# Early-fusion transformer block on one core: in the ending, GpSimd adds the pair ahead's squares later, ScalarE moves squares, VectorE moves low parts

## What is computed

```python
def _ternary_linear(x, w):
    alpha = jnp.mean(jnp.abs(w))
    w_t = jnp.sign(w) * (jnp.abs(w) > 0.5 * alpha).astype(w.dtype)
    w_q = w + jax.lax.stop_gradient(w_t - w)
    rms = jnp.sqrt(jnp.sum(x * x, axis=-1, keepdims=True)) / jnp.sqrt(jnp.asarray(d, x.dtype))
    x_norm = x / (rms + EPS)
    return jnp.einsum('bsd,fd->bsf', x_norm, w_q)
...
h = _L0_tok_ref(x, W_embed, b_embed, pos_embed)
h = jnp.concatenate([h, txt], axis=1)
h = h + _L0_attn_ref(_layernorm(h, axis=-1), Wq, Wk, Wv, Wo, bo)
h = h + _L0_ffn_ref(_layernorm(h, axis=-1), w_up, w_down)
```

## Time and profile before

| what | value |
|---|---|
| median of 3 runs | 1940.74 us (1939.0 to 1941.06) |
| the profiled execution | 1944.63 us, of which the span from first to last instruction is 1942.6 us |
| busy share of the span | TensorE 96%, its weight loads 80%, VectorE 81%, ScalarE 68%, GpSimd 37% |
| chain that ended last, by engine | TensorE 66%, VectorE 21%, ScalarE 7%, issue 5% |
| mean granted TensorE clock | 0.985 |

### The profile page before, as it was taken

The page is one execution under the profiler, slowest core; times in us unless marked ns, Lnnn a source line. Parts: engine busy times, 40 slices in busy tenths (PEclk is TensorE's granted clock), DMA queues, the critical chain, the costliest instruction groups (busy, mean ns, idle before and its releaser), DMA issues.

```text
span 1942.6 us, 57163 instructions
## 1 busy us (share of the span) xinstructions
PE 1855.9 (96%) x24066; PEld 1556.0 (80%) x24066; DVE 1571.8 (81%) x2687; ACT 1311.8 (68%) x1920; POOL 726.2 (37%) x649
## 2 busy tenths in 40 slices
PE   5789999999999999999999999999999999999886
PEld 4668888888888888888888888888888888888765
DVE  4578888888888888888888888888888888888866
ACT  4447776677776676777676777667677667677654
POOL 1123333443433444333444343344433344433333
PEclk8899999999999999999999999999999999999988
DMA  4111122111112111112111111211111211111010
GB/s 142 27 47 30 52 57 57 52 38 36 51 52 57 52 44 42 40 52 57 52 54 39 33 52 56 57 52 38 37 50 52 57 52 50 38 38 40 31 35 25
DMA packets 66102, 93.54 MB, mean 48 GB/s; under 512 B 10082, under 2 KB 59718, under 8 KB 65592
## 3 DMA queue, kind: packets, MB, share of 16 engines
q1 hardware_dynamic: 65848, 89.90, 16.4%
HBM read 45.03 MB, written 14.94 MB: 31 GB/s over the span
## 4 chain that ended last, share of the span: by engine, by line
PE 66%; DVE 21%; ACT 7%; issue 5%; DMA 1%; POOL 1%; SPq 0%; POOLq 0%; ACTq 0%; DVEq 0%
PE dense L352 37%; PE score L352 18%; DVE gl L1029 7%; PE pvps L352 6%; DVE pT_lo L1005 4%; PE dense L409 3%; DVE rs L1015 2%; DVE mx L1057 2%; DVE qm L1071 2%; DVE mx L1059 2%; ACT sq L759 2%; ACT g L751 1%; PE dense L398 1%; ACT vp L784 1%; ACT pT_hi L718 1%
## 5 line engine op out<-in xcount | busy, mean ns | idle before, releaser
L1329 POOL TENSOR_SCALAR_AFFINE_SELECT pr<-pr 114x1368 f32<-114x1368 f32 x190 | 242.7, 1278 | 520.8 <-ACT pr L742 520.7
L742 ACT ACTIVATE pr<-score 114x1824 f32<-114x1824 f32 x190 | 320.8, 1689 | 59.6 <-PE score L352 59.3
L1029 DVE TENSOR_TENSOR gl<-g 128x456 f16<-128x456 f32 x256 | 229.8, 936 | 21.4 <-ACT g L751 20.7
L1341 POOL TENSOR_TENSOR acc<-acc,sq 128x456 f32<-128x456 f32 x190 | 237.4, 1250 | 22.8
L1057 DVE TENSOR_REDUCE mx<-score 114x4 f32<-114x912 f32 x192 | 211.6, 1102 | 30.7 <-PE score L352 30.7
L352 PE MATMUL dense<-wdn,g 128*114 128x256 bf16 x992 | 228.4, 278 | 1.5 <-ACT g L751 1.1
L352 PE MATMUL score<-qm,km 32*114 32x228 f32 (+1 forms) x4096 | 203.9, 324 | 21.3 <-DVE mx L1059 13.3
L352 PE MATMUL dense<-wdn,gl 128*114 128x256 bf16 x992 | 223.2, 273 | 0.0
L352 PEld LDWEIGHTS score<-qm,km 32*114 32x114 f32 x4096 | 157.8, 175 | 66.9 <-issue 57.5
L352 PE MATMUL score<-km,qm 32*114 32x228 f32 (+1 forms) x4096 | 202.6, 323 | 7.0 <-ACT pr L742 7.0
L1015 DVE RECIPROCAL rs<-rs 128x228 f32<-128x228 f32 x128 | 200.6, 1567 | 2.7 <-DMA cxraw<-cxraw 2.7
(11 more groups left out here) (145 smaller groups left out, 4541.5 us busy)
## 6 DMA issues: line engine op xcount, KB each, us to landing
pix<-x SPq DMA_DIRECT2D x32, 588.0 KB
sq<-x SPq DMA_DIRECT2D x32, 588.0 KB
rs<-cxraw SPq DMA_DIRECT2D x256, 57.0 KB, 2.0
cxraw<-cxraw SPq DMA_DIRECT2D x256, 57.0 KB, 2.0
out<-h SPq DMA_DIRECT2D x64, 228.0 KB
h<-txt SPq DMA_DIRECT2D x32, 64.0 KB, 4.6
km<-wqkvo SPq DMA_DIRECT2D x1, 1024.0 KB, 13.9
h<-w_upT SPq DMA_DIRECT2D x1, 1024.0 KB, 14.3
```

The costliest lines, as they stand in the source:

```text
L742: act(probs(pair, q), score[0:R, :, 0:4 * R], ACT.Exp, scale=float(HD) ** -0.5).then_inc(a["exp"], 1)
L1029: tt(gl[:, m], g[:, m], hi_view(g[:, m]), ALU.subtract).then_inc(v["gl"], 1)
L1329: nc.gpsimd.affine_select(out=blocks, in_=blocks, compare_op=ALU.is_ge, fill=0.0, base=0, pattern=[[0, 4], [0, n], [1, R]], channel_multip ...
L1341: tt(acc[:], sq[:, 0] if m == 1 else acc[:], sq[:, m % 4], ALU.add).then_inc(p["acc"], 1)
```

## The change

GpSimd makes variance_powers(L) before all seven accumulate(P), and not between the third and the fourth. VectorE makes all of P's gelu_lo ahead of second_moments(L); low_sums(P) moves behind the low parts of L's columns and the first two gelu_lo(L). ScalarE makes the squares 4 and 5 of P behind `normalized` of L, 6 and 7 behind the high parts, and all eight squares of L behind L's last gelu. TensorE makes sum_squares(P) behind six of L's eight `up` and not behind four.

```diff
@@ TensorE, ending
-                for m in range(4):
+                for m in range(6):
                     up(L, m)
                 sum_squares(P)
-                for m in range(4, 8):
+                for m in range(6, 8):
                     up(L, m)
@@ ScalarE, ending
                 eng.wait_ge(pe["pv"], count(4, L, 3))
-                for m in range(8):
+                for m in range(4):
                     square(P, m)
                 eng.wait_ge(pe["x2t"], count(2, P, 2))
                 normalized(h[0:R, L % 4], xn, sc2[:], nb2, a["xn2"], v["nb2"], L)
+                square(P, 4)
+                square(P, 5)
                 eng.wait_ge(pe["up"], count(8, P, 8))
                 hi_part("x2t", 0, xT2[0], L)
                 hi_part("x2t", 1, xT2[0], L)
+                square(P, 6)
+                square(P, 7)
                 for m in range(8):
                     gelu(L, m)
-                    if 3 <= m < 7:
-                        square(L, m - 3)
-                for m in range(4, 8):
+                for m in range(8):
                     square(L, m)
@@ VectorE, ending
                 gelu_lo(P, 4)
                 gelu_lo(P, 5)
-                second_moments(L)
                 gelu_lo(P, 6)
                 gelu_lo(P, 7)
+                second_moments(L)
                 scale_of(L)
-                low_sums(P)
                 lo_part("x2t", 0, xT2[0], xT2[1], L)
                 lo_part("x2t", 1, xT2[0], xT2[1], L)
-                for m in range(4):
+                gelu_lo(L, 0)
+                gelu_lo(L, 1)
+                low_sums(P)
+                for m in range(2, 5):
                     gelu_lo(L, m)
                 mean_squares(P)
-                for m in range(4, 8):
+                for m in range(5, 8):
                     gelu_lo(L, m)
@@ GpSimd, ending
                 causal(L, 5)
-                for m in range(1, 4):
-                    accumulate(P, m)
                 variance_powers(L)
-                for m in range(4, 8):
+                for m in range(1, 8):
                     accumulate(P, m)
                 accumulate(L, 1)
                 accumulate(L, 2)
```

## The result

The changed kernel takes 1942.70 us in the median of 20 runs (1939.20 to 1945.37), the kernel before 1940.28 us in the median of 20 (1935.46 to 1943.43). The ratio is 1.0015, 95% interval 1.0009 to 1.0022, that is +2.9 us (1.7 to 4.3). The forecast was 1943.4, +2.7 us on the median.

The account below looks back on a forecast made before the run. TensorE, busy 96%, bounds the steady steps; the very end hangs on GpSimd and TensorE nearly alike. Later additions of L (+2.5 us) and slow sum_squares (+0.2) gave +2.7 us on the median, 1943.4 us; range 1940.6 to 1945.6.

Parts of the forecast that it names:

- P's low parts first: VectorE's four gelu_lo of P ahead of second_moments(L): that moves +0.13 us, TensorE's wait shrinks from 4.92 to some 0.5.
- The normalization: L's powers, bias and xn: bias at 1911.6 instead of 1911.79, transposes start 1.7 us earlier.
- The low clock moves: TensorE's idle spell (4.65 us) and low clock shift from P's down matmuls to L's transposes and ups; 1.35 us lost.
- The low part beside an addition: VectorE's low part of L's columns while GpSimd adds P's fifth square: taken as no cost, up to +1.0 us in range.
- The gelus: L's last gelu on ScalarE ends at 1925.05 instead of 1925.34, a net gain of 0.3 us.
- The squares of L: Squares behind L's last gelu: GpSimd's first addition 2.95 us later, fifth done at 1933.4, +2.5 us.
- sum_squares at the low clock: TensorE's sixteen small matmuls at the end, after 3 us of waiting, may run slow: 0 to 0.4 us, 0.2 taken.
- the rival without a low clock: TensorE's clock does not fall or rises at once: +1.1 to +1.3 us, 1941.9; chance 0.17.
- the one with a long one: Low clock stays through most of L's up matmuls, at least until 1921.5: +4.0 us, 1944.7; chance 0.17.
- second_moments is late: Rival: P's two added low parts push second_moments(L) back 1.2 us instead of 0.13: +3.8 us, 1944.5; chance 0.10.
- TensorE sets the end: Rival: TensorE's down of L, not GpSimd's additions, decides the end: -2.2 us, 1938.5; chance 0.08.
- the hold-up behind the powers: VectorE's small operations behind L's powers, held up by a GpSimd addition: 1.10 us for four columns, taken to stay.

Follow-up runs that it names:

- e8: Changed kernel with three of P's GpSimd additions ahead of the powers again; ratio to before 1.0011, end +2.10 us against before.
- e1: Changed kernel with L's squares 0 to 3 between the gelus again, as before; ratio to before 0.9999, end -0.08 us.
- e2: Kernel before with all eight squares of L behind L's last gelu, nothing else changed; ratio to before 1.0012, end +3.07 us.
- e3: Changed kernel with 38 unread matmuls filling TensorE's idle spell ahead of L's transposes; ratio to before 1.0001, end +0.84 us.
- e4: e1 with the 38 unread matmuls of e3 as well; ratio to before 0.9996, end -1.01 us.
- e7: e6 without the unread matmuls; ratio to before 0.9998, end +0.90 us.
- e10: Changed kernel with GpSimd waiting for L's bias before the first of P's additions; ratio to before 1.0002, end +0.63 us.
- e6: e4 with P's root ahead of L's additions, four of these on GpSimd, three on VectorE, sum_squares(L) before the last down part; ratio to before 0.9985.
- e5: Kernel before with 38 unread matmuls in TensorE's idle spell ahead of P's down matmuls; ratio to before 0.9983, 1937.50 us against 1939.94.
- e11: e4 with e10's wait, 22 unread matmuls, L's squares behind gelu 5, sum_squares(P) behind all ups, mean_squares(P) before the last gelu_lo; ratio to before 1.0004.

## Why the prediction was right

Point by point, in times behind the mark:

- *P's low parts first.* Expected: second_moments +0.13 us, wait ahead of P's down 0.5 us at the high clock. Measured: 2.73 against 2.63, +0.10; 0.50 us; clock 1.00.
- *The normalization.* Powers 1.64 us (1.65, the median of before); bias 0.24 us earlier (expected 0.2). Transposes at 12.79 against 14.53: 1.74 us earlier, 1.7 expected.
- *The low clock moves.* The new idle spell is 4.48 us (4.65 expected), and the clock came back 5.2 us after the transposes began (5.15 taken, the middle of two cases; that it came so close is partly luck, as the other traces have 4.0 to 7.2). First up 15.19 against 16.46, -1.27 (-1.2).
- *The low part beside an addition.* Taken at nothing with up to 1.0 us in the range. All 64 took 620 to 634 ns again, the two of L (1911.47 to 1912.80) with GpSimd's additions (1910.27 to 1915.29) beside them:

```profile
L1011 DVE TENSOR_TENSOR xT_lo<-dense,xT_hi x64: 620/631/634, 160.9 to 1912.2; 128x456 f16<-128x456 f32 x64
```

  By the Trainium skill's rule (GPSIMD Engine Reference, section Specifications: contention for instructions with two SBUF inputs or in a two-port mode), this input from PSUM is exempt and gelu_lo is not. The traces agree on both sides: 0.63 here, and 5.14 against 2.25 us for four gelu_lo in e8.
- *The gelus.* The last one ends 0.31 us earlier (0.3).
- *The squares of L.* First addition +2.90 us (+2.95). From its start to the end of the fifth 7.13 us (7.3), before 7.73: fifth addition +2.30 us where +2.5 was written.
- *sum_squares at the low clock.* Taken at 0.2 us, measured at nothing: the clock was still 1.00 after 3.12 us without matmuls. With the 0.2 of the line above this is the whole difference between +2.7 and +2.29.

e1 and e2 show the squares as the cause from both sides, e3 the clock as the second term: 1.45 us, of which 0.33 lies ahead of the first up matmul (14.86 behind the mark in e3, 15.19 in the changed kernel) and 1.12 behind it, where 1.35 was taken. What the sum did not hold is that the two terms overlap: taken one at a time from the changed kernel, 2.37 (e1) and 1.45 (e3), taken together 3.30 (e4).

The number alone would prove little: the range of 1940.6 to 1945.6 also held the rival without a low clock (1941.9) and the one with a long one (1944.7), and the measured interval of 1.7 to 4.3 us even holds the second (+4.0). It is the rows that part them. The clock did fall (0.73 in 1908.00 to 1908.40). The rival that the low clock stays through most of the ups did not come about in the changed kernel's trace, but e7's 7.2 us is close to its 7.5. Of the signs named one failed: P's additions are not one row of seven, since GpSimd waits 1.65 us for P's fifth square behind the third; nothing hung on it. That second_moments is late and that TensorE sets the end are excluded by the rows above. Where the reasoning was thin is the hold-up behind the powers: the prediction had the row (1.10 us for four columns), named its cause, and let it stand as fixed. e10 shows that it could be had for one wait, and e8's expectation went wrong by the same omission.

What stays open: how long the low clock lasts in a given execution. The trace of each kernel is one draw (4.0 and 6.3 us before, 5.8 in e2, 5.2 after, 7.2 in e7), and e2's transposes moved by 0.87 us through it alone. That e6 is faster in the median than its end explains isn't settled either.

## What to carry to other kernels

When work is moved earlier, follow the last consumer and not the first: here the normalization came 1.7 us earlier, but the squares that the final factor needs were queued behind the gelus and came 2.9 us later. An idle spell of TensorE can cost more than the wait, namely matmuls at half pace behind it. The change moved the spell from P's down matmuls to L's transposes and up matmuls, where the slow pace cost 1.45 us (e3). Matmuls that nobody reads, put into the spell of the kernel before, gained 1.46 us in the ending (e5), where the reordering lost 2.29. For an ending of 40 us, measure from a mark inside the trace: the mark itself moved by up to 9.1 us between the traces here, and the edits moved the end by at most 3.1. One trace of each kernel still carries the clock's scatter, 0.87 us in e2.

## What the runs showed of the hardware that was not expected

- Two VectorE operations on 114 x 4 elements with SBUF inputs (0.16 us alone, e10 and e8) took 1.09 and 0.83 us when a GpSimd addition of 128 x 456 f32 had started ahead of them, and each ended as that addition ended (1906.07 and 1906.05, 1907.35 and 1907.33). How long they took was set by what was left of GpSimd's addition and not by their own 0.16 us.
- The clock's fall behind an idle TensorE is no function of the spell's length alone: in the changed kernel it was still at 1.00 when the sums came after 3.12 us without matmuls, and in e3 too, while in e11 a wait of 2.74 us brought 0.50 for the next 4 us and more. In e10, behind a wait of 2.88 us, the eight transposes still ran at 1.00 (1906.00 to 1907.00) and the up matmuls behind them at 0.50 (1908.00 to 1911.00).
